# Adding the residual when each expert's output is stored, loading eight pairs of outputs early, and giving edgeless nodes rows of their own

## What is computed

```
src, dst = edge_index (131072 random edges) and one loop for each node
e = leaky_relu(a_src[src] + a_dst[dst]); alpha = softmax of e over the edges into dst
agg = segment_sum(h[src] * alpha, dst) + b_gat
scores = layernorm(agg).reshape(M, 4, 4).mean(1)
g = softmax over the best two of scores, 0 for the others
for e in range(4):
    hh = gelu(x @ W1[e] + b1[e])            # 256 -> 512
    out = out + g[e] * (hh @ W2[e] + b2[e])  # 512 -> 256
result = x + out
...
B, N, D = (16, 512, 256)
'edge_index': jax.random.randint(ks[6], (2, N_EDGES), 0, B * N, jnp.int32)
```

## Time and profile before

| | us |
|---|---|
| median of three timed runs | 10487.33 (10477.21 to 10490.65) |
| the profiled execution's own time | 10549.46 |
| its span, first to last instruction | 10547.3 |
| expert outputs, from about 8565 to 10210 | 1645 |
| edges' finish, from about 10210 to 10232 | 22 |
| choose and sum, from about 10232 to the end | 315 |

### The profile page before, as it was taken

The page is one execution under the profiler, slowest core; times in us unless marked ns, Lnnn a source line. Parts: engine busy times, 40 slices in busy tenths (PEclk is TensorE's granted clock), DMA queues, the critical chain, the costliest instruction groups (busy, mean ns, idle before and its releaser), DMA issues. The chain is left out here.

```text
span 10547.3 us, 83890 instructions
## 1 busy us (share of the span) xinstructions
PE 7308.9 (69%) x22345; PEld 4293.4 (41%) x22345; DVE 6105.9 (58%) x17158; ACT 3382.3 (32%) x7429; POOL 5112.9 (48%) x5326
## 2 busy tenths in 40 slices
PE   2446655555668999999984566566656369889865
PEld 1322322222335555555562333332333245555544
DVE  9956666666666555555455677777777631222234
ACT  1223333333333333333342333333333331222123
POOL 0066666666651000003436666666666556666622
PEclk9767677777779999999996667767766569999987
DMA  3166665656651000001255566565656532222237
GB/s 115 57 198 186 186 191 183 190 186 188 190 176 50 25 24 25 25 23 33 22 124 172 182 189 187 184 190 186 187 184 189 157 105 52 61 57 54 61 107 236
DMA packets 672268, 1353.98 MB, mean 128 GB/s; under 512 B 203627, under 2 KB 402126, under 8 KB 670898
## 3 DMA queue, kind: packets, MB, share of 16 engines
q0 software_dynamic: 238688, 579.40, 21.8%
q1 hardware_dynamic: 406480, 743.56, 20.2%
q10 hardware_dynamic: 26626, 25.65, 0.7%
HBM read 711.27 MB, written 649.65 MB: 129 GB/s over the span
## 5 line engine op out<-in xcount | busy, mean ns | idle before, releaser
L1371 PE MATMUL g1sm_sump<-g_acc,g1sm_to 128*128 128x264 f32 x3520 | 1549.9, 564 | 1023.9 <-DVE g_acc L1517 647.1
L1371 PE MATMUL g0sm_sump<-g_acc,g0sm_to 128*128 128x260 f32 x3520 | 1506.1, 547 | 1036.1 <-DVE g_acc L1517 403.6
L1261 POOL DMA_INDIRECT g_acc<-htab,g1sm_src x1760 | 1672.5, 950 | 993.0 <-issue 677.3
L1261 POOL DMA_INDIRECT g_acc<-htab,g0sm_src x1740 | 1655.5, 951 | 903.1 <-issue 619.3
L1371 PEld LDWEIGHTS g1sm_sump<-g_acc,g1sm_to 128*128 128x128 f32 x3520 | 744.4, 254 | 1776.9 <-issue 1230.6
L1371 PEld LDWEIGHTS g0sm_sump<-g_acc,g0sm_to 128*128 128x128 f32 x3520 | 716.3, 247 | 1778.7 <-issue 1037.2
L803 POOL DMA_INDIRECT re_rerows<-rtab,re_resrc x1024 | 988.0, 965 | 520.8 <-issue 287.7
L1540 DVE SCALAR_TENSOR_TENSOR g_acc<-g_acc,g0sm_side,g0sm_sump 128x260 f32<-128x260 f32 x1705 | 816.1, 479 | 426.7 <-DMA side<-g_acc 202.4
L2409 DVE SCALAR_TENSOR_TENSOR g_acc<-f_yp,f_wgt,g_acc 128x256 f32<-128x256 f32 x784 | 342.6, 479 | 970.2 <-PE f_yp L2329 879.6
L1290 ACT ACTIVATE g1sm_to<-k_iota,g1sm_side 128x128 f32<-128x128 f32 x1760 | 559.4, 388 | 1029.7 <-DMA side<-g_acc 513.7
L1517 DVE TENSOR_TENSOR g_acc<-g_acc,g0sm_weightp 128x256 f32<-128x256 f32 x1760 | 727.8, 414 | 268.4 <-remote 149.0
(11 more groups left out here) (452 smaller groups left out, 9618.6 us busy)
## 6 DMA issues: line engine op xcount, KB each, us to landing
sums<-g_acc SPq DMA_DIRECT2D x440, 528.0 KB
sums<-g_acc SPq DMA_DIRECT2D x440, 520.0 KB
z<-k_arena SPq DMA_DIRECT2D x96, 512.0 KB
k_arena<-z SPq DMA_DIRECT2D x33, 1024.0 KB
g_acc<-htab,g1sm_src POOLq DMA_INDIRECT x1760
g_acc<-htab,g0sm_src POOLq DMA_INDIRECT x1740
x<-g_acc POOLq DMA_DIRECT2D x48, 512.0 KB, 3.4
re_rerows<-rtab,re_resrc POOLq DMA_INDIRECT x1024
```

Source lines behind the costliest of these rows:

```text
L1261: nc.gpsimd.indirect_dma_start(slot[a][:, u, :], None, table, bass.IndirectOffsetOnAxis(ap=src[a][:, u:u + 1], axis=0)).then_inc(landed[a] ...
L1371: nc.tensor.matmul(sump[u % BANKS][:, 0:W], to[u // LOT % RING][:, u % LOT, :], slot[a][:, u, 0:W], start=True, stop=True).then_inc(summed, 1)
```

## The change

- `expert_outputs` also loads x, 512 KB for a chunk, into one of two places, one chunk ahead. Before the outputs of an expert come, DVE writes b2 + x into the tile (a new instruction of 128x1024), and then adds each PSUM bank to what stands there. `z` thus holds each expert's output plus x. As the gates sum to 1, the weighted sum of the outputs holds x once.
- `choose_and_sum` no longer loads x and has no `begin`: DVE's `add` is now gate 0 times output 0 plus PE's sum, in two instructions for a pair. It has 16 places for z, and a load waits for the `add` 16 pairs before.
- The loads of the first eight pairs, whose places lie in the arena, are issued by SP in the edges' finish, ahead of the store of the last piece.
- POOL writes each node's own number into `endi`, and DVE keeps it where the node has no edges (four more instructions of 128x98). What is gathered there is multiplied by zero later, as before.

```
@@ EdgeSums
-    SPLIT = 22
+    SPLIT = 26
...
+        dve.wait_ge(self.named, 1)
+        link(copy(self.own[:, :], self.endi[:, :]))
+        link(tt(tmpn[:, :], tmpn[:, :], self.own[:, :], ALU.subtract))
+        link(tt(tmpn[:, :], tmpn[:, :], has[:, :], ALU.mult))
+        link(tt(tmpn[:, :], tmpn[:, :], self.own[:, :], ALU.add))
         link(ts(tmpn[:, :], tmpn[:, :], 0.0, None, ALU.max))
         link(copy(self.endi[:, :], tmpn[:, :]))
...
+        nc.gpsimd.iota(self.endi[:, :], [[P, NB]], base=0, channel_multiplier=1).then_inc(self.named, 1)
         pool.wait_ge(self.ready, self.SPLIT)
...
@@ finish
+                    load_first(sp)
                     self.store(sp, NG, col, n)
@@ expert_outputs, SP
                 load(0, CHUNK)
+                load_x(0, CHUNK)
                 edges.load_keys(sp)
...
                         load(i + 1, later)
+                        if i > 0:
+                            sp.wait_ge(raised, i * NE)
+                        load_x(i + 1, later)
@@ expert_outputs, DVE
                         dve.wait_ge(z_free, i * NE + e + 1)
+                        if e == 0:
+                            dve.wait_ge(x_in[i % 2], 16 * (i // 2 + 1))
+                        nc.vector.tensor_tensor(zs[e % 2][:, 0:J, :], x[i % 2][:, 0:J, :],
+                                                b2s[:, e, :].unsqueeze(1).to_broadcast([P, J, DIM]), ALU.add)\
+                          .then_inc(raised, 1)
+                        dve.wait_ge(raised, i * NE + e + 1)
                         for q in range(Q):
                             dve.wait_ge(y_ready, i * (2 * NE) + Q * e + q + 1)
-                            nc.vector.tensor_tensor(zs[e % 2][:, 2 * q:2 * q + 2, :], yp[q][:, :, :],
-                                                    b2s[:, e, :].unsqueeze(1).to_broadcast([P, 2, DIM]), ALU.add)\
-                              .then_inc(y_used, 1)
+                            part = zs[e % 2][:, 2 * q:2 * q + 2, :]
+                            nc.vector.tensor_tensor(part, yp[q][:, :, :], part, ALU.add).then_inc(y_used, 1)
@@ first_outputs (new)
+    def load_first(sp):
+        for n in range(held):
+            sp.dma_start(places[n], zv[:, 2 * n:2 * n + 2, :]).then_inc(z_in[n], 16)
@@ choose_and_sum, SP
-                for n in range(N):
+                for n in range(early, N):
                     s = n % XS
                     if n >= XS:
-                        sp.wait_ge(begun, n - XS + 1)
-                        sp.wait_ge(summed, n - XS + 1)
-                    sp.dma_start(x[s][:, :, :], xv[:, 2 * n:2 * n + 2, :]).then_inc(x_in[s], 16)
-                    sp.dma_start(zs[s], zv[:, 2 * n:2 * n + 2, :]).then_inc(x_in[s], 16)
+                        sp.wait_ge(done, n - XS + 1)
+                    sp.dma_start(zs[s], zv[:, 2 * n:2 * n + 2, :]).then_inc(z_in[s], 16)
@@ choose_and_sum, DVE
-                def begin(n):
...
+                def add(n):
                     s = n % XS
+                    dve.wait_ge(z_in[s], 16 * (n // XS + 1))
                     if n >= YS:
                         dve.wait_ge(stored[n % YS], 16 * (n // YS))
-                    dve.wait_ge(begun, n + 1)
                     dve.wait_ge(summed, n + 1)
-                    tt(y[n % YS][:, :, :], part0[n % YS][:, :, :], rest[n % YS][:, :, :], ALU.add).then_inc(done, 1)
+                    for j in range(2):
+                        m = stt(out=y[n % YS][:, j, :], in0=zs[s][:, j, 0:DIM], scalar=gate[:, 2 * n + j, 0:1],
+                                in1=rest[n % YS][:, j, :], op0=ALU.mult, op1=ALU.add)
+                    m.then_inc(done, 1)
```

More of the change, by code:

```diff
@@ L712, in __init__ @@
         self.first = c.sb("refirst", [P, cols])
-        self.tmpn = c.sb("retmpn", [P, NB])
+        self.tmpn, self.own = c.sb("retmpn", [P, NB]), c.sb("reown", [P, NB])
+        assert NB * P <= P * cols
         self.ad = c.sb("read", [P, most, H])
@@ L725, in __init__ @@
              "piece_done", "kept"))
+        self.named = c.sem("renamed")
         every = self.rows[:, :, :].rearrange("p c w -> p (c w)")
@@ L878, in sums, with finish @@
         assert link.n == self.SUMS
-    def finish(self):
+    def finish(self, load_first):
         nc, K, H, W, D, X, NG = self.nc, self.K, self.H, self.W, self.D, self.X, self.NG
@@ L2460, in expert_weights, with expert_outputs @@
     return w, issue
-def expert_outputs(nc, K, name, turned, z, w, edges, room):
+def expert_outputs(nc, K, name, xin, turned, z, w, edges, room):
     w1s, w2s, b2s, w_in = w["w1s"], w["w2s"], w["b2s"], w["w_in"]
@@ L2475, in expert_outputs @@
     HALF_T = NT // 2
+    after = at + KC * NT
     with Ctx(nc, name) as c:
+        x = [w["rest"][:, after:after + CHUNK * DIM].rearrange("p (j d) -> p j d", j=CHUNK),
+             c.sb("x", [P, CHUNK, DIM])[:, :, :]]
         zs = [outs[:, j, :, :] for j in range(2)]
@@ L2480, in expert_outputs @@
         yp = [c.ps(f"yp{m}", [P, 2, DIM]) for m in range(2)]
-        names = ("h_ready", "h_done", "y_ready", "y_used", "z_ready", "z_free", "stored")
-        h_ready, h_done, y_ready, y_used, z_ready, z_free, stored = (c.sem(n) for n in names)
-        xT_in = [c.sem(f"xT_in{j}") for j in range(2)]
+        names = ("h_ready", "h_done", "y_ready", "y_used", "z_ready", "z_free", "stored", "raised")
+        h_ready, h_done, y_ready, y_used, z_ready, z_free, stored, raised = (c.sem(n) for n in names)
+        xT_in, x_in = ([c.sem(f"{n}{j}") for j in range(2)] for n in ("xT_in", "x_in"))
+        xv = xin.rearrange("(b p) d -> p b d", p=P)
         zv = z.rearrange("(b p) f -> p b f", p=P)
@@ L2620, in _, with first_outputs, choose_and_sum @@
                 step(NCH - 1, LAST, NG - 1, NG // 2 - 1, 1)
-def choose_and_sum(nc, K, name, rsum, endi, has, H, NE, asn, adn, hn, bias, gamma, beta, xin, z, out, arena):
+def first_outputs(nc, c, z, arena):
+    width = 2 * z.shape[1]
+    held = arena.shape[1] // width
+    places = [arena[:, s * width:(s + 1) * width].rearrange("p (j f) -> p j f", j=2) for s in range(held)]
+    z_in = [c.sem(f"z_in{s}") for s in range(held)]
+    zv = z.rearrange("(b p) f -> p b f", p=P)
+    def load_first(sp):
+        for n in range(held):
+            sp.dma_start(places[n], zv[:, 2 * n:2 * n + 2, :]).then_inc(z_in[n], 16)
+    return places, z_in, load_first
+def choose_and_sum(nc, K, name, z_in, early, rsum, endi, has, H, NE, asn, adn, hn, bias, gamma, beta, z, out, arena):
     F, X = H * NE, 2 * H + H * NE
     PARTS = ((0, 8), (8, 24), (24, 56), (56, NB))
-    N, XS, YS, DS, LATE = NB // 2, 12, 4, 2, 2
+    N, XS, YS, DS, LATE = NB // 2, 16, 4, 2, 2
     REST = NODES - (NB - 1) * P
@@ L2641, in choose_and_sum @@
         sc, beat, one = (c.sb(n, [P, most, NE]) for n in ("sc", "beat", "one"))
-        x = [c.sb(f"x{s}", [P, 2, DIM]) for s in range(XS)]
         held = arena.shape[1] // (2 * NE * DIM)
@@ L2685, in _ @@
                     s = n % XS
[L2686 removed]
+                    pe.wait_ge(z_in[s], 16 * (n // XS + 1))
                     pe.wait_ge(spread_ready, n + 1)
@@ L2833, in _ @@
                     for n in range(a // 2, b // 2):
-                        begin(n)
                         if n >= LATE:
@@ L2922, in gnn_two_layers @@
             rsum = dram("rsum", (RE, C))
+            early, z_in, load_first = first_outputs(nc, r, z, arena)
             with Ctx(nc, "re") as e:
@@ L2925, in gnn_two_layers @@
                                  rsum, endi, has)
-                expert_outputs(nc, K, "f1", turned, z, experts, edges, room)
-                edges.finish()
-            choose_and_sum(nc, K, "cs", rsum, endi, has, H, NE, asn, adn, hn, a[f + "b_gat"], a[f + "ln_gamma"],
-                           a[f + "ln_beta"], xs[3], z, out, arena)
+                expert_outputs(nc, K, "f1", xs[3], turned, z, experts, edges, room)
+                edges.finish(load_first)
+            choose_and_sum(nc, K, "cs", z_in, len(early), rsum, endi, has, H, NE, asn, adn, hn, a[f + "b_gat"], a[f + "ln_gamma"],
+                           a[f + "ln_beta"], z, out, arena)
 _INS = ['x', 'src', 'dst', 'L0_gnn_W', 'L0_gnn_att_src', 'L0_gnn_att_dst', 'L0_gnn_bias', 'L0_ffn_Wr', 'L0_ffn_br',
```

20 lines of the change are left out of this document (6 added, 14 removed).

## The result

| | before, us | after, us | ratio (95% interval) |
|---|---|---|---|
| first comparison, 9 runs each | 10483.61 | 10514.75 | 1.0025 (1.0015 to 1.0035) |

The change makes the kernel slower by 0.25%, about 26 us (16 to 37). The prediction said 10491, +4, from a base of 10487; 10514.75 lies 5 us above the top of its range.

A forecast was written before the change was run, and what follows sets the result against it. PE was taken to pace the expert outputs, a dependent chain the finish, late answers then PE the last stage. Residual 0, early loads +15, last stage without x +1, own rows -12 gave +4 on 10487.33: 10491 us, range 10460 to 10510.

The forecast's parts named there:

- The residual in the expert outputs: Expert outputs: 120 us of new DVE additions fit into DVE's free time while PE sets the pace; cost 0.
- Eight loads in the finish: Edges' finish: the last piece's store waits behind 8.39 MB of loads, and gather, merge and scatter move with it; +15 us.
- the early loads bring nothing: Start of the last stage: DVE waits 14.78 us for the first gathers, not for z; gain 0.
- The last stage without x: Last stage: 49 loads of x go, but DVE's add takes 0.88 us a pair instead of 0.69; +1 us.
- no load is waited for in the second half: Last stage after 10373, 45 of 49 pairs: no load is waited for, so sixteen places instead of twelve bring nothing.
- Own rows: Last stage, gathers of blocks 64 to 97: packets return to some 50 ns, late answers end sooner; -12 us.
- late answers: Profile, last stage's first half: instructions' successors start late, such as 1.18 us idle after 0.18 us, until 13 us after the last gather.
- same-row reads hold back the timed runs: Rival, last stage: without late answers, one-row gathers beside loads end 38 us after DVE asks; -22 in all, 10465 us; chance 0.18.
- DVE reaches part 3 at 139 us of the stage: Last stage without late answers: first gathers, gates, 22 pairs of 2.63 us and three starts sum to 139 us.
- 0.88/256*160: Gather queue between 10286 and 10296: one engine's time for a packet, 55 ns, against 534 ns where one row is read.
- Do the late answers exist in the timed runs?: Whole kernel: late answers may belong to the profiled execution alone, which its 62 us above the timed runs allow, not prove.
- The chance of 0.22 for faster: Whole kernel: faster by more than 0.2% (21 us), from most of the same-row case and a third of the store-not-held-back case.

The follow-up runs named there:

- before_again: The kernel before, unchanged, run again on a chip without late answers: ratio 1.0001, 9347.26 us.
- residual_only: The changed kernel without the eight loads in the finish and with the old endi (nodes without edges gather row 131071); without late answers ratio 1.0002, 9348.06 us.
- fewer_gathers: The kernel before, with blocks 64 to 97 set to zero instead of gathered in the last stage; with late answers ratio 0.9968, 10534.50 against 10567.68 us.
- own_rows_only: The kernel before with one part alone, nodes without edges gather their own rows; without late answers ratio 0.9982.

## Why the prediction was wrong by some 22 us

**The residual in the expert outputs, cost 0: right.** L2621 is there with 100 instructions of 120.6 us together, as worked out (120), and PE waits nowhere for it, not even when it is made twice.

**Eight loads in the finish, +15: right in mechanism and size.** The gather came at 24.3 us of the finish, as foretold (25), and the finish grew by 13.3 us. The rule cited from the Trainium skill ("DMA: Bandwidth & Descriptors", "Queues, rings and completion order"), consumption in ring order, agrees with these rows. That the early loads bring nothing was right without late answers (235.9 against 236.4 us) and wrong with them, where they bring 5 us in the first half of the last stage.

**The last stage without x, +1: too small, +3 to +6.** The step that failed is the sentence that no load is waited for in the second half, taken as if nothing else were waited for. No load is, but a store is. The prediction looked at the loads alone, which became fewer; it did not ask what a store meets beside them. With the 1 KB packets of x gone the mean packet of a load takes 151 ns instead of 95, a store takes some 3.2 us instead of fitting under PE's 2.59, and the four places for y then pace the pairs at 3.16 us. The Trainium skill, "DMA: Bandwidth & Descriptors", section "Queues, rings and completion order", states that each DMA engine goes round robin between the queues that it has work for and takes a whole packet, there some 9 to 17 descriptors, from one before it switches. The near equal counts of q1 and q10 in `before_again`, 442 and 410, agree with taking turns, in whatever unit; the 257 of q0 beside them show that not every queue got as many. residual_only shows +4.2 us of it; in after part 2 takes 70.1 us from its gates to those of part 3, in before 64.4, +6; and four places against eight on one chip are 3.3.

**Own rows, -12: wrong here, and this is the main miss.** The step that failed is that the late answers end with the last gather's landing, so that quicker landings shorten them. The landings did become quicker. But with own rows and no early loads DVE's additions go on at 139.5 and 138.6 us of the stage, where before has 139.7: own rows are worth 0 to 1 us. fewer_gathers, in which POOL issues for 42.5 us less, moves this point by 33: what counts is how long POOL issues gathers, not how fast they land. On chips without late answers own rows are worth 17 to 19 us, because there the second part runs while the same-row gathers do. The rival "same-row reads hold back the timed runs" had this price in part: it named the gates of part 3 and 38 us; it is 19, through the stores of y. Its estimate that without late answers and without the price of one row DVE reaches part 3 at 139 us of the stage was met by own_rows_only, 140.2. (Where the prediction writes 0.88/256*160 the share is 0.088; its 55 ns are right.)

**Do the late answers exist in the timed runs?** On the chips of the comparison they do: 34 gathers less took 33 us off timed runs, as much as off the trace. The rule that the prediction cited from the Trainium skill ("NOTIFIC — the notification-queue block", section "7.1 Overflow: three behaviours, one of which stalls the engine") would put them down to the recording, but traces recorded in the same way on the other chips have none, so the rule alone does not explain them here. Whether recording has a part in them on the slower chips stays open. Of the 62 us between the profiled execution and the timed runs, which seemed to speak for it, 46 lie in the stages of summing messages and the first layer's experts (2619.1, 2733.0 and 2200.2 us against 2599.6, 2713.5 and 2193.1 in after), which are the same in both kernels.

By its own terms, corrected, the sum is 0 (residual) + 13 (finish) + 5 (stores of y) + 0 (own rows) - 5 (early loads) = +13, or +15 by the two traces' stages, against +26 (16 to 37) and +15 (5 to 24) measured. The chance of 0.22 for faster rested mostly on same-row reads, which cost something only on the other kind of chip. There the parts add up to about nothing, residual +4, own rows -19, early loads +16, and 1.0000 was measured.

**A version that beats both.** Own rows alone, on top of the kernel before, is 0.998 without late answers. With late answers no part of the change was seen to help the whole (own rows alone was not run there), and fewer gathers in a row do (0.9968), but that kernel relies on where these inputs have no edges.

## What to carry to other kernels

Before a large load is put ahead of a small store in one queue, look for who waits for the store: here eight loads that nobody needed yet cost the chain 13 us, and the other order half of that. Where a queue of loads keeps the DMA engines full, count packets as well as bytes, and ask what the stores beside them wait for. And price a saving at the moment when its consumer asks for it: in after the last gather has landed at 125 us of the stage and DVE asks for it at 225, so a quicker landing is worth nothing.

## What the runs showed of the hardware

- The same program takes 9340 us on some chips and some 10500 on others, at a mean granted clock of 0.87 and 0.80, and the difference is not the clock alone: on the second kind DVE's instructions in a chain follow each other every 1.4 us, with 0.2 us of work each, while POOL issues indirect DMAs back to back, and PE does 48 matmuls in 141 us instead of 242. What makes a chip of either kind stays open. A part can be worth 19 us on one kind and nothing on the other.
- Packets of gathers that all read one row (0.10 MB in 257) take 505 to 534 ns each on average, those of gathers that read a row for each place 23 to 55 ns, and the two other queues on the same engines fall from 393 to 123 GB/s together.
- Two queues that both had work waiting, SP's loads and ACT's stores, got near equal numbers of packets through: 442 and 410 in 12 us, although a pair needs twice as many in the first.
